# Local attention with scores as three products of high and low parts, and the query's inverse norm moved into the exponential

## The reference

```python
q = l2norm(q) * qs
k = l2norm(k) * ksc
q, k = rotary_xpos(q, k)
bq = q.reshape(b, h, w, WINDOW, d) * QK_SCALE
sim = jnp.einsum('bhwid,bhwjd->bhwij', bq, bk)
mask = (i < j) | (i > j + WINDOW) | (j == -1)
sim = jnp.where(mask, -jnp.finfo(sim.dtype).max, sim)
attn = jax.nn.softmax(sim, axis=-1)
out = jnp.einsum('bhwij,bhwjd->bhwid', attn, bv)
```

## Time and profile before

| | us |
|---|---|
| median of 3 runs | 2084.21 (2084.05 to 2084.23) |
| the profiled execution | 2087.22 |
| its span, first to last instruction | 2085.5 |

### The profile page before, as it was taken

The page is one execution under the profiler, slowest core; times in us unless marked ns, Lnnn a source line. Parts: engine busy times, 40 slices in busy tenths (PEclk is TensorE's granted clock), DMA queues, the critical chain, the costliest instruction groups (busy, mean ns, idle before and its releaser), DMA issues. The chain is left out here.

```text
span 2085.5 us, 41715 instructions
## 1 busy us (share of the span) xinstructions
PE 1868.5 (90%) x12960; PEld 1331.2 (64%) x12960; DVE 1525.0 (73%) x4128; ACT 1209.6 (58%) x2501; POOL 956.1 (46%) x797
## 2 busy tenths in 40 slices
PE   5778999999996899999996999689999999699975
PEld 4633333333332688888875888578888887578875
DVE  5667888888881899999985554389999998555424
ACT  3414666666665677777774444267777777444423
POOL 3441222222122577777762333267777776233310
PEclk9868999999998899999998999889999999899988
DMA  5690554554532000000022121300000002212137
GB/s 198 230 190 17 78 73 59 75 73 60 74 47 67 10 29 26 25 25 25 25 66 63 31 60 55 96 14 26 25 25 25 25 25 65 63 31 60 51 124 244
DMA packets 150662, 134.67 MB, mean 65 GB/s; under 512 B 31298, under 2 KB 133118, under 8 KB 150398
## 3 DMA queue, kind: packets, MB, share of 16 engines
q1 hardware_dynamic: 149182, 131.75, 27.0%
q10 hardware_dynamic: 1344, 1.31, 0.3%
HBM read 86.60 MB, written 46.16 MB: 64 GB/s over the span
## 5 line engine op out<-in xcount | busy, mean ns | idle before, releaser
L636 ACT ACTIVATE ca_pr<-ca_pS 128x1024 f32<-128x1024 f32 (+3 forms) x384 | 302.0, 814 | 222.3 <-PE ca_pS L551 178.3
L895 ACT ACTIVATE w_pe<-w_sm,w_nmax 128x256 f32<-128x256 f32 x512 | 253.4, 497 | 140.3 <-DVE w_nmax L1007 140.2
L826 POOL TENSOR_TENSOR w_tsn<-w_qk,w_tab 128x512 f32<-128x512 f32 x124 | 251.9, 2053 | 162.7 <-DVE w_pn L1016 162.7
L470 POOL TENSOR_SCALAR_AFFINE_SELECT ca_pr<-ca_pr 128x256 f32<-128x256 f32 x256 | 104.1, 408 | 402.6 <-ACT ca_pr L636 399.6
L527 PE MATMUL ca_pR<-ca_ks,ca_qs 96*128 96x512 bf16 (+3 forms) x768 | 238.3, 347 | 32.0 <-DVEq L719 13.1
L662 DVE CUSTOM_DVE_ANT_0 ca_masked<-ca_pR,ca_later 128x256 f32<-128x256 f32 (+3 forms) x512 | 237.1, 485 | 35.4 <-PE ca_pR L527 30.7
L527 PEld LDWEIGHTS ca_pR<-ca_ks,ca_qs 96*128 96x128 bf16 x768 | 68.0, 97 | 227.0 <-DVE ca_mx L662 128.6
L1007 DVE CUSTOM_DVE_ANT_0 w_sm<-w_pS,masks 128x256 f32<-128x256 f32 x512 | 185.8, 420 | 20.9 <-PE w_pS L1191 20.9
L666 DVE TENSOR_REDUCE ca_mx<-ca_pR 128x1 f32<-128x512 f32 x256 | 176.0, 688 | 32.6 <-PE ca_pR L527 30.9
L551 PE MATMUL ca_pS<-ca_qs,ca_ks 98*128 98x512 bf16 (+3 forms) x768 | 189.4, 330 | 5.3 <-issue 3.5
L834 POOL TENSOR_TENSOR w_rs<-w_ssc,mhalf 128x16 f32<-128x16 f32 x64 | 187.9, 2935 | 5.4
(11 more groups left out here) (166 smaller groups left out, 4426.6 us busy)
## 6 DMA issues: line engine op xcount, KB each, us to landing
QKP<-p_parts SPq DMA_DIRECT2D x32, 384.0 KB, 2.9
ca_qs<-QKP SPq DMA_DIRECT2D x96, 128.0 KB, 6.5
ca_ks<-QKP SPq DMA_DIRECT2D x96, 128.0 KB, 6.8
w_xt<-X SPq DMA_DIRECT2D x64, 128.0 KB, 2.0
X<-w_x SPq DMA_DIRECT2D x64, 128.0 KB, 1.7
f_hh<-X SPq DMA_DIRECT2D x32, 256.0 KB, 4.9
f_xr<-X SPq DMA_DIRECT2D x16, 512.0 KB, 4.8
X<-f_x SPq DMA_DIRECT2D x16, 512.0 KB, 3.3
```

Of the source, the lines that this page charges most:

```text
L636: act.activation(pr[:, k % 2, pair, :, 0:w], pS[:, pair, :, 0:w], ACT.Exp, scale=CS).then_inc(p_ready, 1)
L826: pool.tensor_tensor(*sines(w, j, z), ALU.mult).then_inc(S["ts_ready"], 1)
L895: ins = act.activation(pe_[:, h], sm[:, n], ACT.Exp, bias=nmax[:, n:n + 1], scale=-1.0, accum_out=sums[:, h:h + 1])
```

## The change

1. The scores. The copies of turned keys and queries (kt, qt) become the high parts (F32R), and DVE subtracts them from what stands in PSUM to give the low parts ktl and qtl (`lo_k`, `lo_q`). A score is the sum of high by high, high by low and low by high. Whatever waited for the copies (kt_copied, qt_copied) on PE now waits for the low parts (kt_lo, qt_lo).
2. The query's norm. `unit` multiplies the keys only (kn, 512 columns for 1024); queries are turned as they come out of the rotation (rr). The scores of a row are then too large by the query's norm, and its inverse (rs) enters as the scale of the exponential. Its bias is minus the row maximum times rs, for four heads in one operation after each half of the maxima; ACT waits for it (bias_ready).
3. `copy_qt` stands ahead of `squares` on ACT. `turn_q` waits for the addition on POOL, no longer for the unit. POOL's addition waits also for the turned queries, and POOL clears ktl once a layer. The mask's fill is -1e25 for -1e30.

```diff
             def exps(w, j, it, hf):
-                act.wait_ge(S["max_ready"], ONE + 2 * (g0 + w) + hf + 1)
+                act.wait_ge(S["bias_ready"], ONE + 2 * (g0 + w) + hf + 1)
...
-                    ins = act.activation(pe_[:, h], sm[:, n], ACT.Exp, bias=nmax[:, n:n + 1], scale=-1.0,
+                    ins = act.activation(pe_[:, h], sm[:, n], ACT.Exp, bias=nmax[:, n:n + 1],
+                                         scale=rs[:, j % 2, h:h + 1],
...
                     copy_kt(*a1)
+                    copy_qt(*a1)
                 if a2:
                     squares(*a2)
-                if a1:
-                    copy_qt(*a1)
...
-                dve.tensor_tensor(qkn[:, :].rearrange("p (h d) -> p h d", d=LD),
-                                  rr[:, :].rearrange("p (h d) -> p h d", d=LD),
-                                  rs[:, j % 2][:, :, None].broadcast_to([P, 2 * LH, LD]), ALU.mult)\
-                   .then_inc(S["qkn_ready"], 1)
+                dve.tensor_tensor(kn[:, :].rearrange("p (h d) -> p h d", d=LD),
+                                  rr[:, INNER:2 * INNER].rearrange("p (h d) -> p h d", d=LD),
+                                  rs[:, j % 2, LH:2 * LH][:, :, None].broadcast_to([P, LH, LD]), ALU.mult)\
+                   .then_inc(S["kn_ready"], 1)
+
+            def lo_k(w, j, it):
+                dve.wait_ge(S["kt_copied"], ONE + g0 + w + 1)
+                dve.tensor_tensor(ktl[:, :, j % 2], pX[:, 1].rearrange("p (c t) -> p c t", c=4),
+                                  kt[:, :, j % 2].bitcast(F32), ALU.subtract).then_inc(S["kt_lo"], 1)
+
+            def lo_q(w, j, it):
+                dve.wait_ge(S["qt_copied"], ONE + g0 + w + 1)
+                dve.tensor_tensor(qtl[:, :, :], pX[:, 3].rearrange("p (c t) -> p c t", c=4),
+                                  qt[:, :, :].bitcast(F32), ALU.subtract).then_inc(S["qt_lo"], 1)
...
-                                                   -1.0, BIG, ALU.add, ALU.min, nmax[:, n:n + 1])
+                                                   1.0, -BIG, ALU.add, ALU.max, smax[:, n:n + 1])
                 ins.then_inc(S["max_ready"], 1)
+
+                dve.wait_ge(S["max_ready"], ONE + 2 * (g0 + w) + hf + 1)
+                dve.scalar_tensor_tensor(nmax[:, 4 * hf:4 * hf + 4].rearrange("p (b s) -> p b s", b=2),
+                                         smax[:, 4 * hf:4 * hf + 4].rearrange("p (b s) -> p b s", b=2), -1.0,
+                                         rs[:, w % 2, 4 * hf:4 * hf + 4].rearrange("p (s b) -> p b s", s=2),
+                                         ALU.mult, ALU.mult).then_inc(S["bias_ready"], 1)
...
                 copy_last(w, j, it)
+                if a1:
+                    lo_k(*a1)
+                    lo_q(*a1)
                 if a2:
                     cosines(*a2)
                     sum_squares(*a2)
...
                 for c in (2 * hf, 2 * hf + 1):
-                    for r in range(2):
-                        rows = slice(r * LD, (r + 1) * LD)
-                        bank, slot = score_place(2 * c + r)
-                        ins = pe.matmul(pS[:, bank, slot], qt[rows, c, :], kt[rows, c].rearrange("p s t -> p (s t)"),
-                                        start=True, stop=True)
+                    for i, (q, k) in enumerate(((qt, kt), (qt, ktl), (qtl, kt))):
+                        for r in range(2):
+                            rows = slice(r * LD, (r + 1) * LD)
+                            bank, slot = score_place(2 * c + r)
+                            ins = pe.matmul(pS[:, bank, slot], q[rows, c, :],
+                                            k[rows, c].rearrange("p s t -> p (s t)"), start=i == 0, stop=i == 2)
```

More of the change, by code:

```diff
@@ L51 @@
 NEG = -1e30
+BLOCKED = -1e25
 WHOLE = HID // P
@@ L211, in _ @@
                 own = kind // 2
-                pool.affine_select(out=m[:, kind, own], in_=m[:, kind, own], compare_op=ALU.is_ge, fill=NEG,
+                pool.affine_select(out=m[:, kind, own], in_=m[:, kind, own], compare_op=ALU.is_ge, fill=BLOCKED,
                                    base=0, pattern=[[-1, P]], channel_multiplier=1).then_inc(masked, 1)
@@ L216, in _ @@
                 if kind:
-                    pool.affine_select(out=prev, in_=prev, compare_op=ALU.is_ge, fill=NEG,
+                    pool.affine_select(out=prev, in_=prev, compare_op=ALU.is_ge, fill=BLOCKED,
                                        base=0, pattern=[[1, P]], channel_multiplier=-1).then_inc(masked, 1)
                 else:
-                    pool.memset(prev, NEG).then_inc(masked, 1)
+                    pool.memset(prev, BLOCKED).then_inc(masked, 1)
         @block.scalar
@@ L740, in phase_window @@
     (wo_st, wo_hi, wo_lo, scales, tab, xt, hs, thi, tlo, qk, sq, ss, ssc, rs,
-     tc, tsn, rr, qkn, v, kt, qt, sm, nmax, sums, rsum, pe_, pn, pt, oth, otl, x1, pX, pS) = W.tensors
+     tc, tsn, rr, kn, v, kt, ktl, qt, qtl, sm, smax, nmax, sums, rsum, pe_, pn, pt, oth, otl, x1, pX, pS) = W.tensors
     qkv_st, qkv_hi, qkv_lo = W.weights
@@ L838, in add @@
                 pool.wait_ge(S["ts_ready"], ONE + 2 * (g0 + w) + 2)
[L839 removed]
+                pool.wait_ge(S["kn_ready"], ONE + g0 + w)
+                pool.wait_ge(S["qt_ready"], ONE + g0 + w)
                 pool.tensor_tensor(rr[:, :], tc[:, :], tsn[:, :], ALU.add).then_inc(S["added"], 1)
@@ L846, in rope @@
                     add(*nxt)
-            pool.memset(kt[:, :, 1], 0.0).then_inc(S["cleared"], 1)
+            pool.memset(kt[:, :, 1].bitcast(F32), 0.0).then_inc(S["cleared"], 1)
+            pool.memset(ktl[:, :, 1].bitcast(F32), 0.0).then_inc(S["cleared"], 1)
             pool.memset(v[:, 3], 0.0).then_inc(S["cleared"], 1)
@@ L924, in copy_qt @@
                    .then_inc(S["qt_copied"], 1)
-            act.wait_ge(S["cleared"], ONE + 2 * layer + 2)
+            act.wait_ge(S["cleared"], ONE + 3 * layer + 3)
             turned(0, 0, 0)
@@ L1047, in _ @@
             unit(0, 0, 0)
+            lo_k(0, 0, 0)
+            lo_q(0, 0, 0)
             cosines(1, 1, 0)
@@ L1198, in _ @@
                 project(w, w, 0)
-            pe.wait_ge(S["cleared"], ONE + 2 * layer + 2)
+            pe.wait_ge(S["cleared"], ONE + 3 * layer + 3)
             turn_k(0, 0, 0)
@@ L1735, in window_tensors @@
         sb("tc", [P, 2 * INNER], F32), sb("tsn", [P, 2 * INNER], F32), sb("rr", [P, 2 * INNER], F32),
-        sb("qkn", [P, 2 * INNER], F32),
-        sb("v", [P, 4, INNER], F32), sb("kt", [P, KI, 2, P], F32), sb("qt", [P, KI, P], F32),
-        sb("sm", [P, LH, 2 * P], F32), sb("nmax", [P, LH], F32), sb("sums", [P, LH], F32), sb("rsum", [P, LH], F32),
+        sb("kn", [P, INNER], F32),
+        sb("v", [P, 4, INNER], F32), sb("kt", [P, KI, 2, P], F32R), sb("ktl", [P, KI, 2, P], F32R),
+        sb("qt", [P, KI, P], F32R), sb("qtl", [P, KI, P], F32R),
+        sb("sm", [P, LH, 2 * P], F32), sb("smax", [P, LH], F32), sb("nmax", [P, LH], F32), sb("sums", [P, LH], F32), sb("rsum", [P, LH], F32),
         sb("pe", [P, LH, 2 * P], F32), sb("pn", [P, LH, 2 * P], F32), sb("pt", [P, 4, 512], F32),
@@ L1790, in program @@
         K.starts = [(x, ONE) for sems in (WS, FS) for v in sems.values() for x in (v if isinstance(v, list) else [v])]
-        K.starts += [(WS["kt_copied"], 1), (WS["exp_done"], 2), (WS["x1_ready"], 2), (WS["ot_lo"], 2),
-                     (WS["qt_copied"], 1), (FS["act_ready"], 2), (FS["x2_ready"], 2)]
+        K.starts += [(WS["kt_lo"], 1), (WS["exp_done"], 2), (WS["x1_ready"], 2), (WS["ot_lo"], 2),
+                     (WS["qt_lo"], 1), (FS["act_ready"], 2), (FS["x2_ready"], 2)]
         made = c.enter_context(nc.semaphore("made"))
```

28 lines of the change are left out of this document (14 added, 14 removed).

## The result

| | before | after |
|---|---|---|
| median, us | 2084.22 | 2301.42 (2298.88 to 2307.9) |
| profiled execution, us | 2087.22 | 2307.9 |
| its span, us | 2085.5 | 2306.2 |
| period of a window in layer 1, mean of 31, us | 12.88 | 16.34 |
| granted clock over the span | 0.950 | 0.929 |

A forecast was written before the change was run, and what follows sets the result against it. It took PE and an equally long loop through POOL and DVE as bounds. The period would grow 2.5 us to 15.4; 60 such periods (150) plus 6 at layer starts gave +156, 2240 us; range 2155 to 2270.

The forecast's parts named there:

- What bounds the kernel: Local attention before the change: PE at its limit, and a loop through POOL and DVE closing in the same 12.88 us.
- Two loops of equal length: PE's work, and sum of squares through POOL, DVE, transposes and ACT to the next sum: 12.88 us a window each.
- the lock: DVE operations with both inputs in SBUF stand until a running POOL operation ends; w_rs holds nothing back for long.
- Bias held: Second bias on DVE, issued at 4.02, held by POOL's addition until about 5.87 us in every window; chance 0.70.
- The first rival: Bias on DVE not held by POOL's addition: period 14.0 us, total 2159 us; chance 0.15.
- Low parts and w_tc: DVE after the key copy: two low parts add 1.22 us; w_tc, not held, costs 1.15 in sequence (1.23 alone).
- Moving the squares: ACT's squares behind the query copy: costed at nothing, about 0.5 us if DVE came sooner.
- Scores: PE: 24 products in pairs take 1.44 us against 1.93, a gain of 0.5, worth nothing while another loop is longer.
- The queries' inverse norm moves into the exponential as a scale: ACT's exponential: scale costed at nothing, at most a few hundredths of a us for each of 8.
- The third rival: Granted clock falls as PE idles some 3 of 15.4 us: far over 2300 us; chance 0.03.
- The second rival: PE is the only limit and DVE's slack takes the new work: 30 us faster, 2054 us; chance 0.04.

The follow-up runs named there:

- e2: Kernel before, with only POOL's addition issued ahead of its inverse norm: 2084.74 us, ratio 0.999.
- e12: Kernel before, only reordered: POOL's addition before its inverse norms, DVE's cosine products before the fourth probabilities copy, POOL's sine products after w_tc: 2086.09 us, ratio 0.999.
- e5: Kernel before plus low parts, three-product scores and query copy ahead of squares; unit, bias and exponential as before: 2167.51 us, ratio 1.039.
- e1: Changed kernel, with only POOL's addition issued ahead of its inverse norm: 2181.34 us, ratio 1.045 to the kernel before.
- e8: Changed kernel, each 128x4 bias operation replaced by four on one column, inverse norm as column operand: 2210.88 us, ratio 1.060 to the kernel before.
- e9: Kernel before plus low parts and three-product scores alone, with POOL's addition first, cosine products before the fourth probabilities copy, sine products after w_tc: 2078.98 us, ratio 0.996.
- e11: Changed kernel with a constant as the exponential's scale instead of the inverse-norm column (results not those of the reference): 2241.78 us, ratio 1.074 to the kernel before.
- e4: Changed kernel plus six unused products of 512 columns a window on PE, around the transposes of the probabilities: 2262.28 us, ratio 1.084 to the kernel before.
- e6: Kernel before plus the query's norm at the exponential alone (scale column, bias operations), full-precision scores, no low parts: 2217.26 us, ratio 1.063.

## Why the prediction was wrong in its time and right in its sign

**What bounds the kernel: right.** Two loops of equal length, and the reading of the lock from the earlier trace rows. e2 and e12 showed that PE alone holds the kernel before, e5 that the other loop takes over as soon as it gets 1.22 us longer.

**Bias held: right, to hundredths.** Counted from the end of the sum of squares (1004.52 + 1.21 = 1005.73): w_rr predicted from 3.43 to 5.82, measured 3.43 to 5.83; second bias issued at 4.02, measured 3.94; fifth exponential at 5.91, measured 5.89. The first rival (2159, bias not held) is out, and e1 and e8 show what a bias that isn't held is worth (81 and 51 us at full clock). The Trainium skill (SBUF — State Buffer, Who interferes with whom) names the property, two SBUF inputs beside a GpSimd instruction that reads SBUF. The trace agrees for this 128x4 operation, and e8 with one input and a column for the other, at 128x1; w_pn at 128x256, also one input and a column, is held beside w_rr (e8). It does not agree for w_rs, beside which the first bias took 0.16 us.

**Low parts and w_tc: right.** Counted back from the end of the next sum, predicted and measured in brackets: key copy -4.21 (-4.18), low keys -3.59 (-3.55), low queries -2.98 (-2.94), w_tc -2.37 (-2.34). w_tc took 1.22 as said. Moving the squares cost nothing.

**Scores: nearly.** 1.44 us predicted, 1004.20 to 1005.83 = 1.63 measured: pairs as said, each 0.12 later than the last, except the first, which took 0.22, and 0.21 at the end. On the changed kernel it counts for nothing, as predicted; it shows only where PE is the limit (e9).

**Where it failed: "The queries' inverse norm moves into the exponential as a scale; I cost that at nothing, since the exponential already takes a bias by row; at most it is a few hundredths for each of 8."** It was 0.093 each. That the bias comes from a column says nothing about a second column, and the bound of a few hundredths was drawn from no row, though the trace of before had one: L1363, with two columns, at 775 ns beside 689 with one. This one term accounts for 59 of the 61 us. Directly it moved the second reciprocal from 8.01 to 8.36 and the undisturbed period from 15.3 (e11) to 15.66: 2262.28 - 2241.78 = 20 us between e4 and e11, both at full clock. Indirectly it let the clock fall in many windows (by the starts of the fourth copy 19 of 31 in layer 1 last over 16 us): 2301.42 - 2262.28 = 39 us between after and e4. The sum: 156 predicted, 20 and 39 make 215 of the 217 us. With the column taken out, e11, the kernel takes 2241.78, 2 us from the forecast.

**The third rival, a falling clock, was put at 0.03 with the words "nothing here sits idle long". That was the wrong question.** The longest wait of PE in the stage is 0.9 us, and the clock falls all the same, in part of each window and not throughout; that is why it cost 39 us and not "far over 2300". The Trainium skill (TensorE: Matmul & The Clock Gate, A second HAM failure mode: psum-queue depth-cycling) tells of a kernel whose clock went back and forth because TensorE paused briefly and often between groups of products. The trace agrees with that picture: three waits of 0.4 to 0.7 us among sixteen transposes, and every drop of the clock about where the last eight of them start. The range ended at 2270 since this case had been left out as a whole, with no price for a clock that falls only now and then.

**The second rival (2054, PE alone) fell** by e5. The rule of the Trainium skill that stood beside it (Perfetto Trace Analysis, Identifying the Most-Contended Engine), by which DVE is the engine to relieve, gave the right sign for the change. e9 speaks against it as a reason: DVE is busy 94% there (327.87 of 350), more than the 92% of before, and the kernel is faster.

## What to carry to other kernels

A small operation with two inputs in SBUF is priced by what the other engine is doing at the moment it is issued, not by its size: put the long operation on the other side of it (e1, 81 us at full clock). Splitting it into operations of one input and a column worked here for 128x1 (e8, 51 us), but w_pn, of the same kind and 256 columns wide, is held. An extra operand of an instruction that runs eight times on the chain is a term of its own: look for a row that has it in the whole trace, in other phases too (here L1363), and where there is none, leave the bound wide. A change that makes the engine of the products wait a little more, in several places close to each other, can cost more than the waits, since its clock may fall: read the clock of single windows of the loop, not only its mean.

## What the runs showed of the hardware

- The clock fell from full to half speed with PE busy 84% of an undisturbed window in after and 90% of the stretch in e6 and no wait over 1.0 us, and not in each window: after has windows of 15.66 and of 17.1 us in irregular rows. Six products that compute nothing kept it at 1.00. The busy share doesn't sort the runs: e11 with 301.61 busy us of 350 stayed at 1.00, e6 with 314.95 did not. All 37 drops in the windows of after and e6 came 2.3 to 2.9 us after the first transpose of the probabilities, behind a wait for the copy of q of 0.75 and 0.73 us in the mean (0.39 in e11). No run changed that wait alone.
- A second column operand costs an activation of 128x256 another 0.093 us (497 to 590 ns), with bias already given by one; at 128x512 the rows of before have 597, 689 and 775 ns with none, one and two.
- The power -1/2 on POOL (w_rs, 2.93 us) holds a DVE operation with two SBUF inputs not at all that could be seen (0.16 us beside it; in e1 the bias was issued 0.17 us after w_rs and took 0.16), while the addition w_rr holds it to within 0.02 us of its end.
- A multiplication with one SBUF input and a column (w_pn, 128x256) issued beside w_rr is held to 0.15 us behind its end (e8); the same kind of operation on 128x1 is not (0.21 us each).
